# One core, a transformer block with a mixture of experts: the opening written anew, and all steps of the other engines placed anew

## The reference, cut to what matters

```
x = embeddings                                  # 8 sequences x 512 tokens x 128
x = x + attention(layernorm(x), WQ, WK, WV)     # causal, one head of 128
x = x + moe(layernorm(x))
x = x + rwkv(layernorm(x))                      # time mixing (a scan) and channel mixing
x = x + moe(layernorm(x))

def moe(x):
    scores = softmax(x @ Wg)                    # 32 experts
    weights, indices = top_k(scores, 4)
    # expert e takes its first 512 pairs of (token, rank):
    y[token] += weight * ((silu(x @ W1[e]) * (x @ W3[e])) @ W2[e])    # hidden width 64
    z = (silu(x @ Ws1) * (x @ Ws3)) @ Ws2       # shared expert, hidden width 128
    return y + z
```

## Time and profile before

| | us |
|---|---|
| three runs, median (lowest to highest) | 825.35 (824.25 to 826.03) |
| the profiled execution | 824.13 |
| its span, first to last instruction | 822.3 |
| TensorE busy | 805.0 |
| VectorE, ScalarE, GpSimd busy | 660.8, 549.5, 592.8 |

### The profile page before, as it was taken

The page is one execution under the profiler, slowest core; times in us unless marked ns, Lnnn a source line. Parts: engine busy times, 40 slices in busy tenths (PEclk is TensorE's granted clock), DMA queues, the critical chain, the costliest instruction groups (busy, mean ns, idle before and its releaser), DMA issues. The chain is left out here.

```text
span 822.3 us, 12577 instructions
## 1 busy us (share of the span) xinstructions
PE 805.0 (98%) x3781; PEld 604.9 (74%) x3781; DVE 660.8 (80%) x1555; ACT 549.5 (67%) x1017; POOL 592.8 (72%) x457
## 2 busy tenths in 40 slices
PE   7899999999999999999999999999999999999998
PEld 4667887667677677777678777777877767788775
DVE  6688677788898888988778888898878799778654
ACT  3477767775768767689375875649666665767553
POOL 3156768668757777589778887678787796867884
PEclk9899999999999999999999999999999999999999
DMA  9052534415244062450535507255262634425562
GB/s 320 24 132 53 124 85 106 103 41 129 53 106 116 9 153 61 106 129 5 133 85 106 128 15 156 53 119 129 60 137 50 140 70 103 106 50 121 114 126 72
DMA packets 49331, 80.73 MB, mean 98 GB/s; under 512 B 3280, under 2 KB 14544, under 8 KB 48880
## 3 DMA queue, kind: packets, MB, share of 16 engines
q1 hardware_dynamic: 48976, 79.72, 42.3%
q10 hardware_dynamic: 288, 0.20, 0.1%
HBM read 75.19 MB, written 4.72 MB: 97 GB/s over the span
## 5 line engine op out<-in xcount | busy, mean ns | idle before, releaser
L535 POOL TENSOR_TENSOR m_h<-m_v,m_wb 128x512 f32<-128x512 f32 x256 | 352.6, 1387 | 137.2 <-DVE m_v L1276 43.4
L627 ACT ACTIVATE m_th<-pa 128x512 f32<-128x512 f32 x229 | 135.7, 594 | 122.2 <-PE pa L900 117.7
L1276 DVE TENSOR_TENSOR m_v<-m_th,pb 128x512 f32<-128x512 f32 x214 | 144.3, 678 | 20.4 <-ACT m_th L627 12.5
L896 PE MATMUL pa<-m_xh,w1h 128*128 128x512 f32 x272 | 145.6, 535 | 0.4 <-DVE m_v L1279 0.4
L797 ACT ACTIVATE m_hh<-m_h 128x512 fp32r<-128x512 f32 x170 | 106.3, 626 | 26.4 <-POOL m_h L535 25.3
L382 DVE TENSOR_TENSOR m_hl<-m_h,m_hh 128x512 fp32r<-128x512 f32 x98 | 86.8, 887 | 39.0 <-ACT m_hh L797 38.8
L382 POOL TENSOR_TENSOR m_hl<-m_h,m_hh 128x512 fp32r<-128x512 f32 x72 | 95.6, 1329 | 29.5 <-ACT m_hh L797 21.0
L896 PE MATMUL pb<-m_xh,w3h 128*128 128x512 f32 x272 | 115.9, 426 | 0.3 <-DVE m_v L1276 0.2
L897 PE MATMUL pa<-m_xh,w1l 128*128 128x512 f32 x272 | 108.4, 399 | 0.0
L897 PE MATMUL pb<-m_xh,w3l 128*128 128x512 f32 x272 | 108.1, 398 | 0.0
L900 PE MATMUL pb<-m_xl,w3h 128*128 128x512 f32 x272 | 108.0, 397 | 0.0
(11 more groups left out here) (274 smaller groups left out, 1635.1 us busy)
## 6 DMA issues: line engine op xcount, KB each, us to landing
m_wb<-w_scratch SPq DMA_DIRECT2D x126, 512.0 KB, 6.8
x_sb<-in_x SPq DMA_DIRECT2D x8, 256.0 KB, 7.2
m_wb<-in_w SPq DMA_DIRECT2D x2, 1024.0 KB, 6.9
x_out<-x_sb SPq DMA_DIRECT2D x7, 256.0 KB, 7.2
u_scratch<-t_u SPq DMA_DIRECT2D x6, 256.0 KB, 2.2
t_u<-u_scratch SPq DMA_DIRECT2D x6, 256.0 KB, 2.7
f_kk<-in_w SPq DMA_DIRECT2D x1, 1024.0 KB, 9.8
w_scratch<-r_wT SPq DMA_DIRECT2D x16, 64.0 KB, 1.5
```

Of the source, the lines that this page charges most:

```text
L535: pool.tensor_tensor(hidden(g, p), gated(g, p), m_wb[:, p % (GRING * GP), :], ALU.mult).then_inc(sig["m_h"], 1)
L627: ins = act.activation(m_th[:, p % 2, :], pa[p % 2][:, :], ACT.Silu)
L896: pe.matmul(ps[:, :], high[:, p, :], xh, start=True, stop=False)
L1276: dve.tensor_tensor(gated(g, p), m_th[:, r, :], pb[r][:, :], ALU.mult).then_inc(sig["m_v"], 1)
```

## The change

- **Low parts.** GpSimd makes those of w1, w3 and w2 for the 16 pairs, in quarters of four pairs (128x512), twelve instructions; VectorE made them in six of 128x1024. VectorE keeps the casts, now w1h and w3h right behind the first normalisation. TensorE waits for the quarter that it needs instead of for all (`c_wl`). The shared expert's parts stay on VectorE.
- **Normalisation of sequence 0 for the router** moves from ScalarE to VectorE, each tile with a signal of its own, and TensorE turns tile by tile; the same signals for attention of sequence 0. The statistics of tiles 0 to 2 are taken before the last tile is ready.
- **Experts chosen on exponentials**: `max` and `match_replace` read r_ex instead of r_p, so that sum, reciprocal and r_p are needed only for the weights (r_ws). The logits of sequence 0 go into py instead of pq.
- **Units 0 and 1** are weighted by VectorE straight from the banks pq and py (`weigh`); ScalarE's two copies and GpSimd's first two products go.
- **Fillers**: `keep_clock` takes its numbers from a table, 49 in all instead of 28.
- **Order**: nearly every tuple of slots, and the tables NATIVE, LOW_ON_POOL and TANH, have other numbers. NATIVE names 102 units before and after, LOW_ON_POOL 102 and then 90 (71 of them split ones, which alone count; 72 before), TANH 43 and then 38.

The diff, cut to its core (of the tuples one line of each kind stands):

```
 NATIVE = (
-    (1, 7, 10),
-    (10,),
+    (0,),
+    (1,),
...
+FILL = (9, 12, 3, 5, 3, 4, 2, 1, 4, 0, 2, 4)
...
-                        sp.wait_ge(sig["c_w"], W_UP)
+                        sp.wait_ge(sig["c_wl"], 2 * QUARTERS - 1 + j)
...
@@ gpsimd @@
                 if g == 0 and p < SPREAD:
-                    pool.wait_ge(sig["c_wbs"], p + 1)
-                elif p % GP == 0 or (g == 0 and p == SPREAD):
+                    return
+                if g == 0 and p == SPREAD:
+                    pool.wait_ge(sig["m_h"], SPREAD)
+                if p % GP == 0 or (g == 0 and p == SPREAD):
                     pool.wait_ge(wb_in[p // GP], 32 * g + 32)
...
-                if slot == (36, 14, 3, 1, 3, 7, 5, 11, 5, 9, 5, 9, 11, 2, 9, 4)[q]:
+                if slot == (34, 13, 16, 2, 6, 10, 7, 9, 6, 3, 11, 10, 7, 1, 2, 4)[q]:
                     rsqrt(r_rs[:, :], r_ve[:, :], "r_vedone", q + 1, "r_rstd")
...
+            def weights_step(slot):
+                w1, w3 = w_stage[:, 0:PAIRS, :], w_stage[:, PAIRS:2 * PAIRS, :]
+                if slot == (5,)[0]:
+                    low_quarter(0, w1l, w1, w1h, 1)
...
+            def low_quarter(i, low, src, high, made):
+                part = quarter(i)
+                pool.wait_ge(sig["c_w"], made)
+                pool.tensor_tensor(low[:, part, :], src[:, part, :], high[:, part, :].bitcast(F32),
+                                   ALU.subtract).then_inc(sig["c_wl"], 1)
...
@@ scalar @@
-                    act.wait_ge(sig["r_nm"], q + 1)
-                    normalise(r_xn, chunk(sequence(q)), r_rs, r_nm, "r_xn")
+                    if q > 0:
+                        act.wait_ge(sig["r_nm"], q)
+                        normalise(r_xn, chunk(sequence(q)), r_rs, r_nm, "r_xn")
...
-            def spread_step(slot):
-                if slot == (39,)[0]:
-                    for p in range(SPREAD):
-                        act.wait_ge(sig["c_wb"], p + 1)
-                        if p == 0:
-                            act.wait_ge(sig["c_w"], W_UP)
-                        act.activation(m_wb[:, p, :], (pq, py)[p % 2][:, :], ACT.Copy).then_inc(sig["c_wbs"], 1)
...
@@ tensor @@
-            def turn(ps, src, signal):
+            def turn(ps, src, signal, by_tile=None):
                 for t in range(T):
+                    if by_tile is not None:
+                        pe.wait_ge(sig[by_tile], t + 1)
                     ins = pe.transpose(ps[:, P * t:P * (t + 1)], src[:, t, :], ident[:, :])
...
+                if g == 0 and p < PAIRS and p % (PAIRS // QUARTERS) == 0:
+                    pe.wait_ge(sig["c_wl"], 2 * (p // (PAIRS // QUARTERS)) + 1)
...
             def probs(n, i, blocks):
-                if n == 0 and i == 2:
-                    keep_clock(2)
+                if n == 0:
+                    keep_clock(FILL[5 + i])
...
@@ vector @@
+                if slot == (16,)[0] and q == 0:
+                    dve.wait_ge(sig["a_add"], 2)
+                    for t in range(T - 1):
+                        dve.bn_stats(r_st[:, t, :], chunk(0)[:, t, :])
...
                     dve.wait_ge(sig["r_rstd"], q + 1)
-                    shifts(r_nm[:, :], r_mv, r_rs[:, :], "r_nm")
+                    if q == 0:
+                        normalise(r_xn, chunk(0), r_mv, r_rs, "r_xn")
+                    else:
+                        shifts(r_nm[:, :], r_mv, r_rs[:, :], "r_nm")
...
-                    dve.wait_ge(sig["r_p"], q + 1)
+                    dve.wait_ge(sig["r_ex"], q + 1)
                     for t in range(T):
-                        ins = dve.max(r_top[:, t, :], r_p[:, t, :])
+                        ins = dve.max(r_top[:, t, :], r_ex[:, t, :])
...
+            def weigh(p):
+                dve.wait_ge(sig["m_v"], p + 1)
+                dve.wait_ge(sig["c_wb"], p + 1)
+                dve.tensor_tensor(hidden(0, p), gated(0, p), (pq, py)[p][:, :], ALU.mult).then_inc(sig["m_h"], 1)
```

More of the change, by code:

```diff
@@ L549, in pro_step @@
                                        ALU.subtract).then_inc(sig["m_xl"], 1)
+            def weights_step(slot):
+                w1, w3 = w_stage[:, 0:PAIRS, :], w_stage[:, PAIRS:2 * PAIRS, :]
+                if slot == (5,)[0]:
+                    low_quarter(0, w1l, w1, w1h, 1)
+                if slot == (5,)[0]:
+                    low_quarter(0, w3l, w3, w3h, 2)
+                if slot == (29,)[0]:
+                    low_quarter(1, w1l, w1, w1h, 1)
+                if slot == (19,)[0]:
+                    low_quarter(1, w3l, w3, w3h, 2)
+                if slot == (25,)[0]:
+                    low_quarter(2, w1l, w1, w1h, 1)
+                if slot == (9,)[0]:
+                    low_quarter(2, w3l, w3, w3h, 2)
+                if slot == (6,)[0]:
+                    low_quarter(3, w1l, w1, w1h, 1)
+                if slot == (9,)[0]:
+                    low_quarter(3, w3l, w3, w3h, 2)
+                if slot == (33,)[0]:
+                    low_quarter(0, w2l, w2_stage, w2h, 3)
+                if slot == (38,)[0]:
+                    low_quarter(1, w2l, w2_stage, w2h, 3)
+                if slot == (25,)[0]:
+                    low_quarter(2, w2l, w2_stage, w2h, 3)
+                if slot == (23,)[0]:
+                    low_quarter(3, w2l, w2_stage, w2h, 3)
@@ L1224, in constants_set, with row_stats @@
                 dve.wait_ge(sig["c_dve"], 7)
-            def row_stats(src, st, mv, n, s_st, s_mv):
-                for t in range(T):
+            def row_stats(src, st, mv, n, s_st, s_mv, first=0):
+                for t in range(first, T):
                     ins = dve.bn_stats(st[:, t, :], src[:, t, :])
@@ L1335, in weights_step @@
-                if slot == (31,)[0]:
-                    low_part(w2l[:, second, :], w2_stage[:, second, :], w2h[:, second, :], 7)
-                if slot == (32,)[0]:
+                if slot == (0,)[0]:
+                    high_part(w1h[:, 0:PAIRS, :], w_stage[:, 0:PAIRS, :], "in_w1")
+                if slot == (0,)[0]:
+                    high_part(w3h[:, 0:PAIRS, :], w_stage[:, PAIRS:2 * PAIRS, :], "in_w3")
+                if slot == (5,)[0]:
+                    high_part(w2h[:, 0:PAIRS, :], w2_stage, "in_w2")
```

426 lines of the change are left out of this document (215 added, 211 removed), and 22 rows, old and new, of the table NATIVE.

## The result

| | before | after |
|---|---|---|
| median of the runs, us (lowest to highest) | 825.22 (824.25 to 826.03) | 817.55 (817.50 to 818.03) |
| the profiled execution's span, us | 822.3 | 815.8 |

The ratio after to before is 0.9908, 95% interval 0.9884 to 0.9931. (One execution of the new kernel, disturbed over its whole length, is left out of the table.) The forecast was 823.3 with a range from 820.4 to 826.6: the sign was right, the size of the gain was about a quarter of the measured one, and the range missed it by 2.9 us. A second group of runs gave 817.83 (816.93 to 818.48) for the same kernel, against 824.76 for the kernel before.

A forecast was written before the change was run, and what follows sets the result against it. The prediction took the time as unit 2's start plus a fixed stream of TensorE matmuls, scattered waits and the tail. Opening -1.6 and tail -0.4 made -2.0 us, from 825.35 to 823.3, range 820.4 to 826.6.

The forecast's parts named there:

- The stream behind 46.64 keeps its length; I take 0 for it.: TensorE's matmuls from unit 2 on: same work as before, so a change of 0.
- The bound that I wrote, -4.3: Scattered waits of TensorE behind unit 2: -4.3 us if none were left, +4.3 if twice as many.
- I let it be low until 37 as now, because TensorE still waits some 1.3 us ahead of the turn.: TensorE's clock in the opening: low until 37, unit 2 at 45.0; 43.75 if it never drops, 46.1 if low throughout.
- Attention of sequence 0: In the opening: its last product at 21.5 instead of 20.40, 1.1 us later.
- The root: Router's reciprocal root on GpSimd behind eleven quarters: from 27.1 to 28.1, ending 2.1 us later than before.
- From the turn to unit 2: Opening, from the router's tiles turned by 29.5 to unit 2 at 45.0, 1.6 us earlier than 46.64.
- so nothing more: Router: choosing on exponentials takes 0.75 us out of the count's way, but the count waits for TensorE, so no gain.
- The tail: Last units: with all last lows on VectorE, unit 16's matmuls start at 816.95 instead of 817.3, 0.4 us earlier.
- B: Rival: 60 activation table loads on ScalarE instead of 54, slower: 831.0 if all six are exposed, 827.2 if half; chance 0.15.
- A: Rival: GpSimd not late or the clock stays up, opening up to 2.2 earlier: -4.2 us, 821.2; chance 0.17.
- C: Rival: opening gives next to nothing, clock low through both units or first attention held: unit 2 at 46.1, 824.9; chance 0.23.
- my last sentence: Wrong if unit 2 starts within 0.5 of the old 46.6, or waits behind it change more than the opening.

The follow-up runs named there:

- new_open_old_rest: The changed kernel with the slots and tables of passes 1 to 15 from the kernel before: 822.05 us, ratio 0.9952 to the kernel before.
- old_fill_all: The kernel before with more fillers everywhere in the opening, 59 in all: 822.70 us, ratio 0.9975 to the kernel before.
- old_open_fill_new_rest: The kernel before's opening and pass 0 with many fillers, experts chosen on exponentials, new numbers from pass 1 on: 818.21 us, ratio 0.9924.
- after_again: The changed kernel run and profiled once more, unaltered; no median given, unit 2 at 42.78 us.
- new_root_early: The changed kernel with three of GpSimd's eleven quarters moved behind the router's root of sequence 0: 820.28 us, ratio 0.9952 to the kernel before.
- new_choice_p: The changed kernel choosing experts on r_p again, sum, reciprocal and r_p ahead of the maximum in seven passes: 821.73 us, ratio 0.9968.
- new_sum_early: The changed kernel, choice on exponentials kept, but sum, reciprocal and r_p placed early, ahead of the maximum: 820.69 us, ratio 0.9954.

## Why the prediction was wrong, step by step

**"The stream behind 46.64 keeps its length; I take 0 for it."** This failed, and is the largest part of the miss. The stream went from 772.3 to 769.6 in the two profiles: 2.7, where 0.4 was forecast for the tail, so 2.3 of the 4.5 that the forecast missed between them. Between kernels with one opening, the new order is worth 4.2 us (`new_open_old_rest`) and 4.5 us (`old_fill_all` to `old_open_fill_new_rest`). Over all profiles the rest took 771.9 to 774.0 in the four with the old order, and 768.8 to 770.7 in the eleven with the new one and its choice on exponentials. The bound that I wrote, -4.3, has the right size, but in part by luck: it stood for no waits left at all, and only 40 to 56% of the waits in brackets went (2.0 to 3.4 us). I took the middle for want of a reason, and left the lower end out of the range. Most of what is missing lies in the waits too, for one costs more than its bracket:

```profile
494.80 0.40 PE L947 MATMUL pa<-m_xl,w1h 128*128 128x512 f32 x1
495.38 0.50 PE L943 MATMUL pb<-m_xh,w3h 128*128 128x512 f32 x1 [0.18 <-DVE m_v L1330]
```

The bracket counts from the recorded end of the matmul ahead, 0.40 behind its start, while an unbroken row starts its next 0.235 behind it. So a wait costs 0.16 more than is written, in both traces. Three waits fewer make 0.5 of the 0.7 missing in the two profiles, and six fewer 1.0 of the 1.2 in each of the other two pairs; 0.2 stays open. Exchanging only the tables of native and low-part units wasn't tried, since they hang together with the numbers of the steps.

**"I let it be low until 37 as now, because TensorE still waits some 1.3 us ahead of the turn."** Both halves failed. The fillers ended at 28.36 instead of 27.15, because attention was later than forecast, and the first tile was ready about 0.7 earlier, because the root was: two errors closed the gap, and the clock stayed at 1.00. (A gap of 0.31 was there in `after_again`, and the clock stayed up too.) With it up, the forecast's own figure for unit 2 was 43.75; it came at 42.85. The deeper error was to read one execution's clock as the kernel's: over many runs the falls cost the kernel before 2.0 us of its median by `old_fill_all` and 3.1 by its executions at full clock, not always the 3 of one profile.

**Attention of sequence 0.** Forecast 1.1 later, measured 1.9: the held cast (1.04) and the held a_ve (1.08) were priced as delays of GpSimd only. The exclusion works both ways, and the one that starts first has it. `after_again` shows the other outcome, 0.9 earlier and no gain from it.

**The root.** Forecast 27.1 to 28.1, measured 26.39 to 27.40. The queue of quarters did set it, as I said; eleven of them start 0.04 closer than one lasts (0.5 in all). r_ve, forecast for 24.06, was ready only at 26.31, held by the quarter just ahead of the root; without the quarters it was 0.17 long (`new_root_early`).

**From the turn to unit 2.** Forecast 15.5 (29.5 to 45.0), measured 13.9 (28.93 to 42.85). Six matmuls of unit 0 at 0.43 instead of 0.235 are 1.2 of that.

**The exponentials, "so nothing more".** Wrong by up to 3.9 (`new_choice_p`), of which some 2.9 is where sum and r_p may stand (`new_sum_early`). I had looked at sequence 0 alone.

**The tail.** Forecast 0.4 earlier, measured 0.3 later (from the last up product to the last row 5.68 instead of 5.42). A low part on VectorE beside GpSimd took 0.97 for 0.69, and unit 16's product (m_h, then m_hh) behind it was as much later:

```profile
807.61 0.97 DVE L384 TENSOR_TENSOR m_hl<-m_h,m_hh 128x512 fp32r<-128x512 f32 x1 [1.26 <-ACT m_hh L839]
...
809.93 0.47 PE L976 MATMUL py<-m_hh,w2h 128*128 128x512 f32 x1 [0.26 <-ACT m_hh L839]
```

**The rivals.** B did not happen as a whole: there are 60 table loads, as forecast, and no row behind unit 2 shows TensorE waiting for m_th. ScalarE waited for TensorE ahead of silu 112.6 us in 93 waits where it was 117.7 in 91, so the cover held nearly everywhere:

```profile
ACT m_th L676 <- PE pa L947: 112.6, 93, 4.6
```

A piece of it did happen. The longest wait of the new stream, the 0.90 at 80.09, is for a turned block that ScalarE copies behind a table load and an exponential, and I had looked for the loads' price only at m_th:

```profile
77.07 1.28 ACT L717 ACT_TABLE_LOAD   x1 [2.15 <-PE pu L1064]
78.36 0.69 ACT L717 ACTIVATE a_p<-pv,a_nm 128x512 f32<-128x512 f32 x1
...
79.56 0.48 ACT L724 ACTIVATE a_pT<-pu 128x384 f32<-128x384 f32 x1
```

A had the clock right and the wrong reason: GpSimd was late. I gave it 0.17 and worked it out only as a gain of 2.2 in the opening. C's premise, a clock low through both units, is what the kernel before's profile shows, and nearly two thirds of its executions have a mean clock below 0.999; the new kernel's two profiles and nine undisturbed executions don't have it.

**Of what would show it:** the root near 27 (26.4) and unit 1's matmuls 0.235 apart were there; a gap ahead of the turn, the last product near 21.5 (22.34), unit 2 near 45 and waits near 4 were not, and the two quarters near 2.3 only by half: in this profile the cast was the one held, in `after_again` the quarter. By the letter of my last sentence neither sign of being wrong came up: the waits changed by 2.0, the opening by 3.8. In the medians, with the clock's falls taken out, the order behind the opening moved more than all else together.

## What to carry to other kernels

When every step of a tuned stream is placed anew, don't forecast the stream at zero because the work is the same: take its scattered waits as what the change can win, each a little dearer than its bracket, and put the whole bound in the range. Before a stretch at a low clock is taken as a property of a kernel, look whether its run times spread; a kernel whose times lie 8 us apart is not described by one profile. And a step moved off the critical path on a shared resource (a quarter on GpSimd) is only harmless beside instructions that don't need that resource; ask it of each new neighbour, not of the queue alone.

## What the runs showed of the hardware

- VectorE and GpSimd exclude each other by instruction, for some kinds of VectorE instructions, and the one issued first goes first; a small instruction is held for as long as a large one. A 128x4 TENSOR_SCALAR of 0.17 took 1.25, four 128x128 ones of 1.12 in all took 3.99, a quarter of 1.27 took 2.30 beside a cast. Beside quarters, bn_stats (three in 0.68 at 21.90), reductions from PSUM, MAX8 and MATCH_REPLACE8 (0.18 each near 32.6) kept their times, and so did a TENSOR_SCALAR on a single column (0.15 at 18.67). The Trainium skill, "SBUF — State Buffer", section "SBUF: two separate sides", names two kinds of VectorE instructions that take the lock, those in a two-port mode and those with two inputs in SBUF; the two-input instructions held here agree with it; the casts and TENSOR_SCALARs do if they ran in that mode, which no row shows.
- The same TensorE work with the same idle gap (0.23 busy of 26 to 28) was followed by a granted clock of 0.50 in one execution and 1.00 in another. A fall costs 2.9 us here, by two profiles and by the two halves of `new_root_early`.
- The cast of w3h, which waits for the same transfer at the same place, began between 9.71 and 10.03 us in eleven profiles of kernels with the new opening, and at 10.74, after a wait of 1.07 for the transfer, in one.
